# Vision tower on one core: three stage boundaries without a barrier

## What is computed

```python
h = patches(x) @ W + b
h = h + L0_attn(_layernorm(h))     # softmax attention, q, k, v, proj
h = h + L0_ffn(_layernorm(h))      # 16 experts, top 2, and a shared expert
h = h + L1_attn(_layernorm(h))     # linear attention
h = h + L1_ffn(_layernorm(h))      # router bits, 12-head attention, MLP, low-rank update
h = h + L2_attn(_layernorm(h))     # selective scan over 192 x 16 states
h = h + L2_ffn(_layernorm(h))      # 128 experts, top 6
h = h + L3_attn(_layernorm(h))     # 12-head attention, top-k scores
h = h + L3_ffn(_layernorm(h))      # 16 experts, first one always, 3 routed
```

## Time and profile before

| | |
|---|---|
| Runs of the kernel before | 841.58 us median of 3 (841.23 to 847.27) |
| The profiled execution | 840.98 us, of which the span from first to last instruction is 839.2 us |
| Busy PE / PEld | 747.5 us (89%) / 559.4 us (67%) |
| Busy DVE / ACT / POOL | 378.3 / 307.3 / 276.0 us |
| Mean granted TensorE clock | 0.934 of full speed (2.4 GHz) |
| Time that engines sat idle until the barrier of L162 released them | PE 7.4 us, 6 times; ACT 50.4 us, 6 times |

### The profile page before, as it was taken

The page is one execution under the profiler, slowest core; times in us unless marked ns, Lnnn a source line. Parts: engine busy times, 40 slices in busy tenths (PEclk is TensorE's granted clock), DMA queues, the critical chain, the costliest instruction groups (busy, mean ns, idle before and its releaser), DMA issues. The chain is left out here.

```text
span 839.2 us, 15814 instructions
## 1 busy us (share of the span) xinstructions
PE 747.5 (89%) x5369; PEld 559.4 (67%) x5369; DVE 378.3 (45%) x1109; ACT 307.3 (37%) x723; POOL 276.0 (33%) x318
## 2 busy tenths in 40 slices
PE   8997999898998998999987999997798968889883
PEld 5675898476576656999754788882356656666662
DVE  1354222224263138888677222221144496555543
ACT  2440222223455227666241222222234354425430
POOL 0004455100002006777112553533301053135772
PEclk9996999887989999999999999999999879879997
DMA  9914899400000033221023789625664040721224
GB/s 350 344 33 163 278 289 300 126 1 1 1 2 2 1 145 122 77 70 32 1 75 103 229 288 390 208 59 177 222 142 160 3 125 3 289 69 47 69 70 108
DMA packets 39253, 108.49 MB, mean 129 GB/s; under 512 B 5616, under 2 KB 12736, under 8 KB 38672
## 3 DMA queue, kind: packets, MB, share of 16 engines
q1 hardware_dynamic: 31584, 88.35, 30.6%
q0 software_dynamic: 7600, 19.25, 8.7%
HBM read 95.88 MB, written 11.70 MB: 128 GB/s over the span
## 5 line engine op out<-in xcount | busy, mean ns | idle before, releaser
L1431 POOL TENSOR_TENSOR ssm_w_low<-ssm_wbc,ssm_w_high 128x512 fp32r<-128x512 f32 x24 | 31.1, 1299 | 38.5 <-ACT ssm_w_high L1386 38.5
L157 ACT ACT_TABLE_LOAD x19 | 24.4, 1283 | 50.6 <-PEq L162 50.4
L2056 POOL TENSOR_TENSOR L_s_up<-L_s_hid,L_s_up 116x288 f32<-116x288 f32 (+1 forms) x10 | 8.3, 830 | 103.8 <-ACT L_s_up L2050 103.8
L1836 DVE TENSOR_TENSOR L_act_many<-L_hid,bank 116x384 f32<-116x384 f32 x28 | 15.5, 554 | 52.9 <-ACT L_hid L1716 52.9
L1346 PE MATMUL bank<-ssm_x_high,ssm_w_high 128*128 128x288 f32 x96 | 33.8, 352 | 3.8 <-DVE bank L1474 2.3
L1441 POOL TENSOR_TENSOR ssm_grown<-ssm_less,xn 128x576 f32<-128x576 f32 x23 | 32.9, 1430 | 8.0 <-ACT ssm_less L1414 5.3
L1691 POOL DMA_INDIRECT y_rows_L<-L_many_y,L_many_rows_out x21 | 20.7, 987 | 40.3 <-ACT L_many_y L1734 32.1
L1716 ACT ACTIVATE L_hid<-bank 116x384 f32<-116x384 f32 x28 | 13.8, 491 | 52.5 <-PE bank L1767 52.5
L1480 DVE TENSOR_TENSOR_SCAN ssm_state<-ssm_decay,bank 128x576 f32<-128x576 f32 x24 | 32.5, 1354 | 0.8
L2025 PE MATMUL bank<-xn,par_L1f 128*116 128x288 f32 (+1 forms) x128 | 31.1, 456 | 0.0
L1666 POOL DMA_INDIRECT L_many_xr<-x_rows_L,L_many_rows_in x27 | 26.8, 994 | 11.9 <-POOL L_many_rows_in L1680 5.7
(11 more groups left out here) (552 smaller groups left out, 1947.5 us busy)
## 6 DMA issues: line engine op xcount, KB each, us to landing
L_w<-in_L2w SPq DMA_DIRECT2D x14, 696.0 KB, 6.5
L_more<-in_L2w SPq DMA_DIRECT2D x10, 696.0 KB, 6.6
L_w<-in_L0w SPq DMA_DIRECT2D x12, 576.0 KB, 4.1
ssm_wbc<-in_wBC SPq DMA_DIRECT2D x24, 256.0 KB, 2.7
L_w<-in_L3w SPq DMA_DIRECT2D x5, 1152.0 KB, 13.5
L_w<-in_L2w SPq DMA_DIRECT2D x14, 384.0 KB, 5.0
L_more<-in_L0w SPq DMA_DIRECT2D x9, 576.0 KB, 4.5
second<-in_L3w SPq DMA_DIRECT2D x16, 291.0 KB, 3.7
```

The source lines that it names most:

```text
L157: self.nc.scalar.activation(self.unread[:, at:at + 1], self.p["ones"][:, 0:1], func)
L1431: pool.tensor_tensor(w_low[t % NW][:, :], wbc[t % NW][:, :], w_high[t % NW][:, :], ALU.subtract).then_inc(low, 1)
```

## The change

load_all no longer has a block of its own: layer0_attention calls it with its own block. layer1_block and selective_scan share a block, and so do layer3_attention and the L3 stage. Three block ends and three calls of T.end_layer go. The first norm behind each of the three boundaries gets first=h_in, a semaphore that the last four writes of h count up. In load_all u now runs over plane inside half, so that half 0 of h is finished first. The waits that the barrier gave are written out: const before ACT, PE and POOL go on; zero_set before the zero rows are stored; h_in >= 4 on SP before the scan's weights, and on SP and POOL before the loads and clears of the L3 routing; PE waits for second.folded there. The two wake calls at the ends of feed_forward and layer3_attention go. store_output, which wasn't used, goes too.

```diff
-def load_all(T):
+def load_all(T, ctx, block):
...
-            dve.memset(T.zero[:, :], 0.0)
+        dve.memset(T.zero[:, :], 0.0).then_inc(T.zero_set, 1)
...
             for u in range(4):
-                    m, at = u // 2, HALF * (u % 2)
+                m, at = u % 2, HALF * (u // 2)
...
+        pe.wait_ge(T.loaded["const"], 16)
...
+            act.activation(T.h[:, m, s:s + HALF], T.bank[u][:, 0:HALF], ACT.Identity,
+                           bias=T.p["tokb"][:, m:m + 1]).then_inc(h_in, 1)
+        act.wait_ge(T.loaded["const"], 16)
+
+    @block.gpsimd
+    def _(pool):
+        pool.wait_ge(T.loaded["const"], 16)
+        pool.wait_ge(h_in, 4)
+
+    return h_in
...
 def layer0_attention(T, ctx, block):
+    h_in = load_all(T, ctx, block)
+
     def first_loads(sp):
+        sp.wait_ge(T.zero_set, 1)
...
-    norm = Norm(T, "L0a_ln", T.h, T.xn, ctx, func=ACT.Exp)
+    norm = Norm(T, "L0a_ln", T.h, T.xn, ctx, func=ACT.Exp, first=h_in)
...
-        wake(T, T.bank[0], BRIDGE // 2)
...
-                dve.tensor_tensor(T.h[:, m, at(s)], T.h[:, m, at(s)], up_bank[s][m][:, 0:HALF], ALU.add)
+                dve.tensor_tensor(T.h[:, m, at(s)], T.h[:, m, at(s)], up_bank[s][m][:, 0:HALF], ALU.add).then_inc(h_out, 1)
...
-def selective_scan(T):
+def selective_scan(T, block, h_in):
...
-        norm = Norm(T, "L2a_ln", T.h, xs, ctx, (relu, mag), func=ACT.Exp)
-        block = ctx.enter_context(nc.Block())
+        norm = Norm(T, "L2a_ln", T.h, xs, ctx, (relu, mag), func=ACT.Exp, first=h_in)
...
         @block.sync
         def _(sp):
+            sp.wait_ge(h_in, 4)
             for t in range(n_tiles):
...
         if common:
+            sp.wait_ge(h_in, 4)
             common.load(sp)
             X.load(sp)
...
     def _(pe):
+        if common:
+            pe.wait_ge(T.folded, E - 1)
         norm.pe(pe)
...
         if common:
+            pool.wait_ge(h_in, 4)
             link = chained(pool, padded)
...
-            wake(T, T.bank[7], BRIDGE // 2)
...
-                                             ALU.add, ALU.add)
+                                             ALU.add, ALU.add).then_inc(h_in, 1)
...
+        experts(T, "L0", layer0_attention)
         T.end_layer()
+        with nc.Block() as block:
+            h_in = layer1_block(T, block)
+            selective_scan(T, block, h_in)
+        T.end_layer()
+        experts(T, "L2")
+        T.end_layer()
...
+        with nc.Block() as block:
+            h_in = layer3_attention(T, block)
+            experts(T, "L3", None, block, h_in)
+        T.end_layer()
```

More of the change, by code:

```diff
@@ L202, in chained @@
     return link
-def load_all(T):
+def load_all(T, ctx, block):
     nc = T.nc
[L208 to L212, removed]
-        block = ctx.enter_context(nc.Block())
[L214 to L229, removed]
-            dve.memset(T.zero[:, :], 0.0)
[L231 to L244, removed]
-                    m, at = u // 2, HALF * (u % 2)
[L246 to L252, removed]
-            for u in range(4):
[L254 to L257, removed]
@@ new lines, in load_all, with _ @@
+    wtok = ctx.enter_context(nc.sbuf_tensor("patches", [128, PATCH_K, TOKENS], F32))
+    chunk_in = [T.sem(f"patches_in{k}") for k in range(PATCH_K)]
+    ones_set = T.sem("ones_set")
+    products = T.sem("tok_products")
+    h_in = T.sem("tok_h_in")
+    T.zero_set = T.sem("zero_set")
+    W = cols(T.p["tokW"], PATCH_K)
+    @block.sync
+    def _(sp):
+        for k in range(PATCH_K):
+            at = slice(256 * k, WIDTHS["tok"] if k == PATCH_K - 1 else 256 * k + 256)
+            sp.dma_start(T.packed["tok"][:, at], T.dram["tok"][:, at]).then_inc(chunk_in[k], 16)
+            sp.dma_start(wtok[:, k, :], T.dram["patches"][:, k, :]).then_inc(chunk_in[k], 16)
+        for g in GROUPS:
+            if g != "tok":
+                sp.dma_start(T.packed[g][:, :], T.dram[g]).then_inc(T.loaded[g], 16)
+        sp.wait_ge(T.loaded["const"], 16)
@@ new lines, in _ @@
+    @block.vector
+    def _(dve):
+        dve.memset(T.xn[:, 0, 0:512], 1.0).then_inc(ones_set, 1)
+        dve.memset(T.zero[:, :], 0.0).then_inc(T.zero_set, 1)
+        dve.wait_ge(T.loaded["const"], 16)
+        dve.tensor_copy(T.ones_bf[:, :], T.p["ones"])
+        dve.tensor_copy(T.before_bf[:, :], T.p["before"])
+        dve.tensor_copy(T.iota_bf[:, :], T.p["iota_r"])
+        for k, to in T.rows_bf.items():
+            dve.tensor_copy(to[:, :, :], spread(T.p["iota"][:, 0:R], 2, k))
+    @block.tensor
@@ new lines, in _ @@
+    def _(pe):
+        pe.wait_ge(ones_set, 1)
+        pe.matmul(T.bank[7][:, :], T.xn[:, 0, 0:128], T.xn[:, 0, 0:512], start=True, stop=True)
+        for k in range(PATCH_K):
+            pe.wait_ge(chunk_in[k], 32)
+            for u in range(4):
+                m, at = u % 2, HALF * (u // 2)
+                mm = pe.matmul(T.bank[u][:, 0:HALF], W[:, k, 128 * m:128 * m + 128], wtok[:, k, at:at + HALF],
+                               start=(k == 0), stop=(k == PATCH_K - 1))
+                if k == PATCH_K - 1:
+                    mm.then_inc(products, 1)
+        pe.wait_ge(T.loaded["const"], 16)
@@ L260, in wake, with _ @@
+    @block.scalar
+    def _(act):
+        for u in range(4):
+            m, s = u % 2, HALF * (u // 2)
+            act.wait_ge(products, u + 1)
+            act.activation(T.h[:, m, s:s + HALF], T.bank[u][:, 0:HALF], ACT.Identity,
[6 more added lines that the diff above has]
+    return h_in
 def wake(T, bank, n):
@@ L2299, in pe, with experts @@
         wake(T, T.bank[7], BRIDGE // 2)
-def experts(T, key, attention=None):
+def experts(T, key, attention=None, block=None, h_in=None):
     with ExitStack() as ctx:
@@ L2314, in experts @@
                 X.blocks = NormedBlocks(X, of_route)
-            block = of_route.enter_context(T.nc.Block())
-            route(X, of_route, block, attention(T, of_route, block) if attention else None)
+            if block is None:
+                block = of_route.enter_context(T.nc.Block())
+            route(X, of_route, block, attention(T, of_route, block) if attention else h_in)
             if key == "L3":
@@ L3342, in layer3_attention @@
         norm = Norm(T, "L3a_ln", T.h, T.xn, ctx, func=ACT.Exp)
-        made = T.sem("a3_out_made")
-        block = ctx.enter_context(nc.Block())
+        made, h_in = T.sem("a3_out_made"), T.sem("a3_h_in")
+        T.folded = second.folded
         ready = head_projections(T, block, "a3_proj", norm, T.xn, w, cols(T.full["av"], 2), qk, p["aqkb"], v, wide, None, second)
@@ L3407, with build @@
-STAGES = ["tok", "L0", "L1", "L2a", "L2f", "L3a", "L3f"]
-def build(nc, dram, stages=STAGES):
+                                             ALU.add, ALU.add).then_inc(h_in, 1)
+        return h_in
+def build(nc, dram):
     with ExitStack() as ctx:
         T = Tower(nc, ctx, dram)
-        load_all(T)
+        experts(T, "L0", layer0_attention)
         T.end_layer()
[L3415 to L3427, removed]
+        with nc.Block() as block:
[4 more added lines that the diff above has]
+        T.end_layer()
+        m = MOE["L3"]
+        T.second = ctx.enter_context(nc.sbuf_tensor("second", [128, m["experts"], m["chunks"] * (DIM + 2)], F32))
+        with nc.Block() as block:
+            h_in = layer3_attention(T, block)
+            experts(T, "L3", None, block, h_in)
+        T.end_layer()
```

10 lines of the change are left out of this document (5 added, 5 removed).

## The result

The changed kernel takes 833.87 us (median of 22 runs, 827.9 to 842.48); the kernel before, on the same chip, 841.40 us (22 runs, 835.7 to 847.61). The ratio is 0.9906, 95% interval 0.9887 to 0.9926: 0.94% faster, or 7.9 us of 841.58, with 1.7 to either side. The forecast was 7.2 us, 834.4.

A forecast was written before the change was run, and what follows sets the result against it. TensorE, busy for 89% of the span, was taken as the bound, losing time at three barriers. The boundaries' -1.2 - 4.0 - 2.0 = -7.2 us against the median 841.58 gave 834.4 us, range 830.5 to 840.0.

The forecast's parts named there:

- First boundary, -1.2: Patches to layer 0: the mean follows the last product, and the first square comes 1.2 us earlier, at about 20.3.
- rival B: First boundary: ScalarE's table load becomes the bound and the boundary gives nothing; 835.6 us, chance 0.05.
- The order of u itself costs nothing: First boundary: writing u half by half uses the same matmuls in other banks, so no cost.
- The zero rows: First boundary: SyncE's zero-row writes go several us earlier; a delay must exceed 9 us to be felt, taken as 0.
- Second boundary, start: -2.49 and 0.1 for VectorE: Layer 1 to scan: the mean starts at 302.71 instead of 305.20, less 0.1 us lost to VectorE's small instructions.
- Second boundary, clock: -1.64: Scan's norm: without the gap the clock stays at 1.00, and mean to first xn takes 5.76 us instead of 7.40.
- Third boundary, -2.0: Layer 3 attention to routing: last add to centring falls from 3.05 to 1.04 us.
- rival C: Whole kernel: clock falls move with the earlier start; 831.1 us if two low stretches shorten (chance 0.20), 836.0 if one is added.
- A: Second boundary: the clock falls in the scan's norm all the same, costing 1.64 us; 836.0 us, chance 0.17.
- D: Scan: it begins in a low clock and stays there; 32 us of low clock would give 850.4 us, chance 0.05.
- E: All three boundaries: SyncE's transfers set the pace, so only their shift of 4.3 us counts; 837.3 us, chance 0.05.

The follow-up runs named there:

- e10: Changed kernel with the first layer's products and evictions in the old order and means waiting for all four evictions; products' end to first square 2.80 us, not 1.96.
- e7: The changed kernel again, all three boundaries joined, on the chip of the single-boundary runs; median 837.8 us, ratio 0.9873 to the kernel before.
- e1: Changed kernel with only the first boundary (patches to layer 0) joined, the other two barriers kept; median 840.5 us, ratio 0.9944 to the kernel before.
- e4: Changed kernel with first and third boundaries joined and the second barrier kept; median 840.0 us, ratio 0.9949 to the kernel before.
- e6: Changed kernel with GpSimd clearing semaphores of each stage's first half early, ahead of the barrier; ratio 0.9887 to the kernel before.
- e8: Changed kernel with the two dropped TensorE fillers kept; last add to centring 2.09 us at the second boundary and 1.90 at the third.
- e2: Changed kernel with only the second boundary (layer 1 to the scan) joined; median 843.8 us, ratio 0.9977 to the kernel before.
- e3: Changed kernel with only the third boundary (layer 3 attention to routing) joined; median 846.3 us, ratio 1.0001 to the kernel before.
- e5: Kernel before with 98 unused semaphores added in the scan's stage; last add to centring behind the scan 4.54 us instead of 3.85.
- e9: Changed kernel with early clears and each stage's semaphores taken from the lowest free numbers; 832.0 us on the other chip, ratio 0.9887 to the kernel before.

## Why the prediction was right, and where it was not

- **First boundary, -1.2: measured -1.36.** The means were not held by the evictions, as forecast, and start 0.16 us before the products' end and not at it (the ends of products in a row are modelled, and the next products overlap them); that is the difference. The table load followed the evictions and ended at 19.72, and the square started 0.09 later than behind centring elsewhere (19.84 - 18.96 = 0.88 against 0.79 in e10 and in the kernel before). So ScalarE did set the start of the square, by 0.09 us. Against rival B, the load took 1.28 us with no time before it. The Trainium skill, ScalarE: Activation LUTs, section What ACT_TABLE_LOAD costs, adds a drain of some 1.38; neither this row nor e10's shows one.
- **"The order of u itself costs nothing".** It costs nothing, and with the wait by halves it brings 0.84 (e10). The forecast had used it, with half 0 complete at 17.8, without giving it a price.
- **The zero rows.** They leave ahead of the barrier's old place, six of them from 14.81 on. They land 17.7 us after issue now and 12.8 before, but L0a lands in 8.2 (8.7 before), as forecast, and xn is followed at once by its products.
- **Second boundary, start: -2.49 and 0.1 for VectorE.** Measured: 1.35 us from mean to centring instead of 1.25, so 0.1 exactly. The start was right.
- **Second boundary, clock: -1.64.** This step failed in its size. "I take it whole" was argued from one execution in which the clock fell, and from two norms that ran at the full pace; the norm whose mean starts at 192.95 in the same trace, with no barrier ahead, did not. Over seven executions the clock fell twice, so the term is at most about -0.5. The bound at nothing, which the forecast gave too, holds for most executions.
- **Third boundary, -2.0: measured -2.00.** c_shift was issued at 704.48 and landed 4.0 us later; its reader ran at 710.96, behind xn.
- **Not in the sum:** the clears, +1.0 us. The prediction named every queue that the change touches, and left out that `end_layer` does work in proportion to what it ends.
- **The total.** Without the clock the change is worth 4.8 us by the distances and 5.6 ± 1.3 by the runs, where the forecast had 5.6. It had 1.6 for the clock; the runs of e7 have 3.5. The forecast of 7.2 for a measured 7.9 thus had two terms wrong in one direction (1.1 too much for the clock at that place, 1.0 given back) and lacked one in the other, which it had only as the good side of rival C. That the number came out so near is in part luck: by the distances and the 0.5 alone it would have been 5.3. Rivals A and D are not seen in any trace, and B only with the 0.09; E falls with the 4.03 that arrived at the scan.

**Rival C and what stays open.** Kernels with the first barrier removed ran at a mean granted clock of 0.9400 (e1, e4, e6 to e8, 47 runs), those that keep it at 0.9346 (before, e2, e3, e5, 79 runs on the same chip): 0.0054 more, ± 0.0019, which at 5.5 us for 0.01 is 3.0 us. On the other chip e9 had 0.9410 in six runs and the kernel before 0.9355 in ten. It goes with the first boundary and with neither of the others. The ten-microsecond windows show one place where it may come from, in layer 0's routing. Before:

```profile
70.00:80.00 10.00, 6.56 (x23) 4.88 (x22) 2.45 (x7) 0.00 (x0) 4.88 (x7) 0.67 0.38 127
80.00:90.00 10.00, 10.00 (x80) 9.05 (x80) 1.95 (x4) 1.90 (x4) 3.67 (x5) 0.83 0.66 209
```

After:

```profile
70.00:80.00 10.00, 5.46 (x31) 4.42 (x31) 1.51 (x4) 0.00 (x0) 5.07 (x7) 0.83 0.27 88
80.00:90.00 10.00, 10.00 (x91) 9.28 (x88) 2.85 (x6) 2.74 (x6) 3.25 (x5) 1.00 0.81 260
```

But e6, e9 and e10, which have the change at this boundary too, had low stretches there much as before (0.67 in the first of the two windows in all three). Layer 1's second norm is another such place: its mean was quick in three of the nine traces without the first barrier, and in none of the five with it, which is too few to tell. The runs show that the clock is higher on average, not why; no kernel was run that shifts the start of the work by itself. The Trainium skill, TensorE: Matmul & The Clock Gate, section What's actually happening, has the gate's judgement run free of the kernel's start. That fits a fall that comes and goes in one kernel at one place; it does not explain a shift of the mean.

## What to carry to other kernels

Joining two stages won 1.4 to 2.4 us at each boundary here. For that the next norm had to wait on halves of its input, at the first boundary the halves had to be written in the order in which they are wanted, and at the other two the filler had to go. Count what the remaining barriers inherit, above all semaphores to clear. An idle engine can clear them early if each stage's numbers stay in few unbroken rows; the distances show that gain, the totals are too coarse for it. A clock level seen in one profile is a draw: look for the same situation elsewhere in the trace, weigh it over several executions before it enters a sum whole, and compare small changes at equal granted clock.

## What the runs showed of the hardware that was not expected

- Clearing semaphores takes GpSimd time on the path: 0.08 us for 8, 0.22 for 36, 0.57 for 100, 0.79 for 138. The drain ahead of it grew with their number too, 0.11 us at 36 and 0.24 at 134. Numbers in broken ranges took a drain and a clear for each range (e6).
- Within one kernel the device time ran over 10 us (the changed kernel, 827.9 to 837.85) and went with the mean granted clock of the execution: 5.5 us for 0.01. That spread is larger than the whole effect studied here.
- After an idle time of the same 1.36 us on TensorE the clock fell in some executions and stayed in others, and in 11 of 14 it was low in layer 1's second norm, which follows the products before it without a gap.
